# The last feed-forward computes its routed experts only for the chosen pairs, with rows moved by indirect transfers

## The reference, cut to what matters

```
g = x @ sw1.T; u = x @ sw2.T                     # 256 -> 1024 each
shared_out = silu(g) * u @ sw3.T                 # 1024 -> 256
scores = sigmoid(x @ router_w.T)                 # 8 experts
_, top_idx = top_k(scores + expert_bias, 2)
top_scores = scores[top_idx] / (sum + 1e-9)
h12 = einsum('td,ehd->teh', x, w12)              # every expert: 256 -> 128 gate, 128 up
out_e = einsum('teh,edh->ted', silu(h1) * h2, w3)
return shared_out + einsum('ted,te->td', out_e, combine)
```

## Time and profile before

| | us |
|---|---|
| median of 3 runs | 2937.14 (2932.88 to 2939.26) |
| the profiled execution, own time | 2938.26 |
| its span in the trace | 2936.5 |
| gating phase (first work to first work of `l3f`) | 2528.1 to 2565.7 |
| `l3f` | 2565.7 to 2927.5 |
| last transfer and end | 2927.5 to 2936.5 |

### The profile page before, as it was taken

The page is one execution under the profiler, slowest core; times in us unless marked ns, Lnnn a source line. Parts: engine busy times, 40 slices in busy tenths (PEclk is TensorE's granted clock), DMA queues, the critical chain, the costliest instruction groups (busy, mean ns, idle before and its releaser), DMA issues. The chain is left out here.

```text
span 2936.5 us, 38100 instructions
## 1 busy us (share of the span) xinstructions
PE 2489.6 (85%) x11114; PEld 1536.4 (52%) x11141; DVE 1415.7 (48%) x3448; ACT 1055.4 (36%) x3161; POOL 580.9 (20%) x832
## 2 busy tenths in 40 slices
PE   4959999999688688869999999994445888599998
PEld 2437676676455344436666566662223455466665
DVE  4951111111355477746656666666775676511111
ACT  1022222222255255535555555552222555221111
POOL 3712222222132200033333333320000000001100
PEclk8959999999899799989999999997666999699999
DMA  7000000000300000000000000002000000000000
GB/s 275 0 7 6 6 5 5 8 5 3 129 1 0 3 1 0 0 6 1 0 0 0 0 0 0 0 0 102 0 0 3 6 4 4 1 1 0 0 0 29
DMA packets 20484, 44.81 MB, mean 15 GB/s; under 512 B 3520, under 2 KB 16192, under 8 KB 19008
## 3 DMA queue, kind: packets, MB, share of 16 engines
q1 hardware_dynamic: 20416, 43.98, 4.1%
HBM read 41.87 MB, written 2.10 MB: 15 GB/s over the span
## 5 line engine op out<-in xcount | busy, mean ns | idle before, releaser
L808 DVE TENSOR_TENSOR moe_hid<-moe_act_g,moe_pU 128x384 f32<-128x384 f32 x128 | 70.9, 554 | 443.5 <-ACT moe_act_g L780 443.5
L780 ACT ACTIVATE moe_act_g<-moe_pG 128x384 f32<-128x384 f32 x128 | 62.8, 490 | 424.6 <-PE moe_pU L735 424.6
L735 PE MATMUL moe_pG<-big,moe_xT 128*128 128x384 f32 x512 | 187.5, 489 | 4.1 <-POOL moe_xT L702 4.1
L1939 ACT ACTIVATE l2x_prob<-l2x_pS,l2x_nb,l2x_rms_q 128x256 f32<-128x256 f32 x256 | 142.5, 566 | 133.4 <-DVE l2x_nb L2087 133.4
L714 POOL TENSOR_TENSOR moe_hidw<-moe_hid,moe_data_w_all 128x384 f32<-128x384 f32 x128 | 105.7, 826 | 426.8 <-DVE moe_hid L808 420.0
L756 PE MATMUL moe_pO<-big,moe_hT 128*128 128x256 f32 x768 | 186.8, 379 | 0.0
L735 PE MATMUL moe_pU<-big,moe_xT 128*128 128x384 f32 x512 | 186.4, 487 | 0.0
L967 PE MATMUL l2x_pQ<-big,l2x_xT 128*128 128x512 f32 x320 | 155.2, 608 | 13.7 <-POOL l2x_cT L2016 10.9
L756 PEld LDWEIGHTS moe_pO<-big,moe_hT 128*128 128x128 f32 x768 | 136.0, 190 | 13.2
L780 ACT ACTIVATE l3f_act_g<-l3f_pG 128x512 f32<-128x512 f32 x64 | 38.2, 597 | 285.9 <-PE l3f_pU L735 285.9
L2084 DVE TENSOR_REDUCE l2x_negmax<-l2x_pS 128x2 f32<-128x512 f32 x128 | 87.8, 686 | 98.1 <-PE l2x_pS L1828 95.3
(11 more groups left out here) (419 smaller groups left out, 5215.5 us busy)
## 6 DMA issues: line engine op xcount, KB each, us to landing
big<-in_e_gate SPq DMA_DIRECT2D x1, 3072.0 KB, 20.8
big<-in_e_up SPq DMA_DIRECT2D x1, 3072.0 KB, 20.7
big<-in_e_down SPq DMA_DIRECT2D x1, 3072.0 KB, 27.7
moe_lanes<-in_l2f_lanes SPq DMA_DIRECT2D x16, 192.0 KB, 2.8
x_all<-in_x SPq DMA_DIRECT2D x1, 2048.0 KB, 8.3
hyena_aT<-in_ctx SPq DMA_DIRECT2D x4, 512.0 KB, 6.8
hyena_toep_rev<-in_k_rev SPq DMA_DIRECT2D x1, 2048.0 KB, 14.1
big<-in_l_wq SPq DMA_DIRECT2D x1, 2048.0 KB, 7.7
```

Source lines behind the costliest of these rows:

```text
L735: last = pe.matmul(ps[:, 0:chunk], lhsT=xT[p][:, k, :], rhs=w(k, c), start=(k == 0), stop=(k == KC - 1))
L780: act.activation(act_g[c % 2][:], pG[c % 2][:, 0:chunk], ACT.Silu).then_inc(silu_done, 1)
L1939: ins = act.activation(prob[g % 2][:, h, :], pS[j][:, (h % 2) * 2 * P:(h % 2 + 1) * 2 * P], ACT.Exp, scale=rms_q[g][:, h:h + 1], bias=nb[: ...
```

## The change

Phases 1 to 3 become one phase, `phase_l3_ffn`. The shared feed-forward is 64 items of a sequence and a chunk of 256 hidden columns, gate and up side by side in one 512-column product (`f_gu`). Each routed item is a tile of 128 rows that all belong to one expert. There are NT = (4096 + 8 x 127) // 128 = 39 such tiles, whatever the data is. The order of items is fixed: 32 shared items (sequences 0 to 7), 39 routed, 32 shared (sequences 8 to 15). One loop step q of TensorE is: `up(q)`, `turn_routed` of the tile two steps ahead, `turn_hidden(q-1)`, `down(q-2)`; ScalarE and VectorE have matching orders.

Routing runs between the early items: logits at q = 2 to 5, exponential and scores at 6, the two choices at 7 and 8, ranks by matmul at 9 (32 small bf16 matmuls), each row's slot at 10, the owner of each tile at 11, the weights at 12. A DRAM buffer `route_x` of 39 x 128 rows of 1 KB is zeroed. GpSimd then scatters the normalised rows to it by 32 indirect transfers (sequence, choice), 128 rows each. SyncE waits for all 32 and loads the tiles, eight ahead. TensorE reads the tile's owner into a register (`value_load`) and takes the expert's weights at that address. The result goes through `y` to a second buffer, `route_y`. When all 39 tiles are stored, GpSimd gathers two rows per token back by 32 indirect transfers into `yk` (four sequences deep). VectorE's `combine` adds both, weighted; each sequence is then stored by itself. The layer norm keeps all 16 normalised tiles (`XN` = B). Every loop is written out; there is no `Fori` left in this step.

```diff
-def phase_gating3(nc, D, G):
-    NE = 8
-    with Phase(nc, "gate3") as ph:
...
+class NormKept(NormAll):
+    XN = B
...
+    NE, TOPK, CH, NC = 8, 2, 256, 4
+    NT = (B * P * TOPK + NE * (P - 1)) // P
+    EARLY = B // 2
+    FLOOR, XR, YR, GR = -3.0e38, 8, 3, 4
+    items = ([("shared", b, c) for b in range(EARLY) for c in range(NC)] + [("routed", j, 0) for j in range(NT)]
+             + [("shared", b, c) for b in range(EARLY, B) for c in range(NC)])
+    Q, R0 = len(items), EARLY * NC
+    R1 = R0 + NT
+    group = {0: range(4, 8), 1: range(8, 12), 2: range(12, 16)}
+    front = [("x", b) for b in range(4)]
...
+        @block.sync
+        def _(sp):
+            def load(j):
+                sp.dma_start(xg[j % XR][:], dx[j * P:(j + 1) * P, :]).then_inc(xg_in[j % XR], 16)
...
+            sp.dma_start(bias[:], D["L3_expert_bias"].partition_broadcast(P)).then_inc(const_in, 16)
...
+            sp.dma_start(lower[:].bitcast(U16), D["c_lower"]).then_inc(const_in, 16)
+            sp.dma_start(onesb[:].bitcast(U16), D["c_onesb"]).then_inc(const_in, 16)
+            sp.wait_ge(cleared, 1)
+            sp.dma_start(dx.rearrange("(j p) c -> p j c", p=P), zero[:].unsqueeze(1).to_broadcast([P, NT, C])
+                         ).then_inc(zeroed, 16)
+            sp.wait_ge(scattered, 16 * TOPK * B)
+            for j in range(XR):
+                load(j)
+            for j in range(NT):
+                sp.wait_ge(out_read, outs["routed", j] + 1)
+                sp.dma_start(dy[j * P:(j + 1) * P, :], y[j % YR][:]).then_inc(y_out[j % YR], 16)
+                if j + XR < NT:
+                    sp.wait_ge(turned, at["routed", j] + 1)
+                    load(j + XR)
+            for b in range(B):
+                sp.wait_ge(combined, b + 1)
+                sp.dma_start(out[b], G["x_all"][:, b, :]).then_inc(stored, 16)
+            sp.wait_ge(stored, 16 * B)
 
         @block.gpsimd
         def _(pool):
-            front_pool(pool)
-        @block.sync
-        def _(sp):
-            sp.dma_start(bias[:], D["L3_expert_bias"].partition_broadcast(P)).then_inc(const_in, 16)
+            for g in range(B // nm.GROUP):
+                nm.pool(pool, g)
+            pool.wait_ge(zeroed, 16)
+            pool.wait_ge(slotted, 1)
+            for b in range(B):
+                for k in range(TOPK):
+                    pool.indirect_dma_start(dx, bass.IndirectOffsetOnAxis(slot_i[:, k, b:b + 1], 0), nm.xn[b][:],
+                                            None).then_inc(scattered, 16)
+            for r in range(YR):
+                pool.wait_ge(y_out[r], 16 * len(range(r, NT, YR)))
+            for b in range(B):
+                if b >= GR:
+                    pool.wait_ge(combined, b - GR + 1)
+                for k in range(TOPK):
+                    pool.indirect_dma_start(yk[b % GR][:, k, :], None, dy,
+                                            bass.IndirectOffsetOnAxis(slot_i[:, k, b:b + 1], 0)
+                                            ).then_inc(yk_in[b % GR], 16)
         @block.tensor
...
+            def turn_routed(j):
+                bank = place(at["routed", j])
+                pe.wait_ge(xg_in[j % XR], 16 * (j // XR + 1))
+                for k in range(KC):
+                    last = pe.transpose(bank[:, k * P:(k + 1) * P], xg[j % XR][:, k * P:(k + 1) * P], G["ident"][:])
+                last.then_inc(turned, 1)
+            def turn_hidden(q):
+                bank = place(at["hidden", q])
+                _, n = sources(q)
+                pe.wait_ge(hid_done, q + 1)
+                for k in range(n // P):
+                    last = pe.transpose(bank[:, k * P:(k + 1) * P], hid[q % 2][:, k * P:(k + 1) * P], G["ident"][:])
+                last.then_inc(turned, 1)
+            def up(q):
+                kind, i, c = items[q]
+                xT, n = sources(q)
+                if kind == "shared":
+                    cols = slice(2 * CH * c, 2 * CH * (c + 1))
+                    pe.wait_ge(turn_read, at["x", i] + 1)
+                else:
+                    if i == 0:
+                        pe.wait_ge(owners, 1)
+                    expert[i] = pe.value_load(owner_i[0:1, i:i + 1], min_val=0, max_val=NE - 1)
+                    cols = bass.ds(expert[i] * CH + 2 * CH * NC, CH)
+                    pe.wait_ge(turn_read, at["routed", i] + 1)
+                if q >= 3:
+                    pe.wait_ge(hid_done, q - 2)
+                for k in range(KC):
+                    last = pe.matmul(pA[q % 3][:, 0:2 * n], lhsT=xT[k], rhs=W["f_gu"][:, k, cols], start=(k == 0),
+                                     stop=(k == KC - 1))
+                last.then_inc(gu_ps, 1)
+            def down(q):
+                kind, i, c = items[q]
+                o, n = outs[kind, i], sources(q)[1] // P
+                pe.wait_ge(turn_read, at["hidden", q] + 1)
+                if c == 0 and o >= 2:
+                    pe.wait_ge(out_read, o - 1)
+                for k in range(n):
+                    if kind == "shared":
+                        w = W["f_down"][:, c * n + k, :]
+                    else:
+                        w = W["f_down"].rearrange("p k c -> p (k c)")[:, bass.ds(expert[i] * C + C * NC * CH // P, C)]
+                    last = pe.matmul(pO[o % 2][:, 0:C], lhsT=hT[q % 2][:, k, :], rhs=w, start=(c == 0 and k == 0),
+                                     stop=(q == lastq[kind, i] and k == n - 1))
+                last.then_inc(down_done, 1)
...
+            def ranks():
+                n = B * NE
+                pe.wait_ge(const_in, 16 * 6)
+                pe.wait_ge(chosen, 1)
+                pe.matmul(pL[:, n:2 * n], lhsT=lower[:], rhs=selb[:], start=True, stop=True)
+                for d in range(1, B):
+                    pe.matmul(pL[:, n + d * NE:2 * n], lhsT=onesb[:], rhs=selb[:, 0:n - d * NE], start=False, stop=True,
+                              skip_group_check=True)
+                for b in range(B):
+                    last = pe.matmul(pL[:, 2 * n:2 * n + NE], lhsT=onesb[:], rhs=selb[:, b * NE:(b + 1) * NE],
+                                     start=(b == 0), stop=(b == B - 1))
+                last.then_inc(ranked, 1)
...
+            for q in range(Q + 2):
+                if q < Q:
+                    up(q)
+                if R0 <= q + 2 < R1:
+                    turn_routed(q + 2 - R0)
+                if 0 < q <= Q:
+                    turn_hidden(q - 1)
+                for b in group.get(q, ()):
+                    turn_x(b)
+                if q in (2, 3, 4, 5):
+                    for b in range(4 * (q - 2), 4 * (q - 1)):
+                        scores(b)
+                if q == 9:
+                    ranks()
+                if q >= 2:
+                    down(q - 2)
 
         @block.scalar
...
+            def evict_routed(j):
+                t = at["routed", j]
+                act.wait_ge(turned, t + 1)
+                if j >= 2:
+                    act.wait_ge(gu_ps, R0 + j - 1)
+                act.activation(xgT[j % 2][:].rearrange("p k t -> p (k t)"), pT[t % 2][:, 0:C],
+                               ACT.Copy).then_inc(turn_read, 1)
+            def evict_hidden(q):
+                t, n = at["hidden", q], sources(q)[1]
+                act.wait_ge(turned, t + 1)
+                if q >= 2:
+                    act.wait_ge(down_done, q - 1)
+                act.activation(hT[q % 2][:].rearrange("p k t -> p (k t)")[:, 0:n], pT[t % 2][:, 0:n],
+                               ACT.Copy).then_inc(turn_read, 1)
+            def silu(q):
+                _, n = sources(q)
+                act.wait_ge(gu_ps, q + 1)
+                if q >= 2:
+                    act.wait_ge(hid_done, q - 1)
+                act.activation(act_g[q % 2][:, 0:n], pA[q % 3][:, 0:n], ACT.Silu).then_inc(silu_done, 1)
+            for b in range(4):
+                evict_x(b)
+            for q in range(Q + 1):
+                if q < Q:
+                    silu(q)
+                if R0 <= q + 2 < R1:
+                    evict_routed(q + 2 - R0)
+                if q > 0:
...
+                if q == 6:
+                    act.wait_ge(logits, B)
+                    act.activation(score[:].rearrange("p b e -> p (b e)"), pL[:, 0:B * NE], ACT.Exp,
+                                   scale=-1.0).then_inc(exp_done, 1)
...
+            def route_choose(k):
+                counts = count[:].unsqueeze(1).to_broadcast([P, B, NE])
+                ch(dve.tensor_reduce(red[:], pick[:], AX.X, ALU.max))
+                ch(dve.tensor_tensor(coded[:], pick[:], bc(red[:], NE), ALU.is_ge))
+                ch(dve.tensor_tensor(coded[:], coded[:], counts, ALU.mult))
+                ch(dve.tensor_reduce(red[:], coded[:], AX.X, ALU.min))
+                ch(dve.tensor_tensor(per_expert(sel[:, k, :]), counts, bc(red[:], NE), ALU.is_equal))
...
+            def gated(q):
+                _, n = sources(q)
+                dve.wait_ge(silu_done, q + 1)
+                if q >= 2:
```

(50 more changed lines are left out.)

197 lines of the change are left out of this document (143 added, 54 removed).

## The result

The changed kernel takes 2823.28 us (median of 4 runs, 2822.25 to 2831.67), beside 2935.01 us of the kernel before in the same comparison (4 runs, 2930.67 to 2939.26). The ratio is 0.9629, with a 95% interval of 0.9609 to 0.9649: faster, but by 112 us where 205 were forecast, and 23 us above the upper end of the range.

The account below looks back on a forecast made before the run. TensorE's matmuls were taken to bound the kernel. The stage summed as 144 to the tiles' end + 48.3 late items + 4.7 wait + 2 hitches + 4 tail = 203 us for 408.4, giving 2732 us, range 2695 to 2800.

Parts of the forecast that it names:

- one step of the ring: Old feed-forward loop on TensorE: matmuls and transposes of one step, put at 5.60 us, 64 steps 358 us.
- matmuls removed: TensorE's columns in the stage: 358 us of matmuls become 135, at 1.51 us a shared item and 0.98 a routed tile.
- slots: Routing among the early shared items: the rows' slots are ready 42 us after the phase's start.
- pace of the scatter p: GpSimd's time per indirect transfer, taken as 1.3 us, between 0.4 and 2.1.
- standstill in the scatter: Before the first routed tile: TensorE stands 15 us for scattered data, plus 2 us for the fallen clock.
- a tile: Routed items: TensorE needs 0.98 us, with ScalarE and register loading 1.3 us each, 51 us for 39.
- wait of the first combine: Start of the late shared items: VectorE, and TensorE with it, waits 4.7 us for the first gathered sequence.
- The front: From the phase's start to the slots: norms, nine steps, logits, routing operations and ranks, 42 us in sum.
- rival 1: Scatter and gather: indirect transfers go one after another or nearly so, from 1.7 us each; 2778 us at 2.1; chance 0.20.
- rival 4: Scatter and gather: GpSimd makes addresses row by row so slowly the kernel gets slower; 2963 us at 5 us each; chance 0.04.
- rival 2: Scatter: hidden behind the shared items, at most 0.84 us a transfer; 2713 us at 0.43; chance 0.12.
- Rival 3: Routed tiles: the register load stops TensorE in every tile, 2.3 us a tile, 39 us more, 2771 us; chance 0.12.

Follow-up runs that it names:

- e2_pairs: The changed kernel, but GpSimd waits for both landings after every two scatters; 2817.64 us, ratio 0.961.
- e10_half_up_eights: The changed kernel with scatters in groups of eight and one of the two gate-and-up products of each shared item left out; 2768.39 us (one run).
- e6_eights: The changed kernel, but GpSimd waits for all landings after every eight scatters; 2796.21 us (one run), timed again 2805.51 us, ratio 0.9553.
- e3_direct_pool: The changed kernel with its 32 indirect scatters replaced by 32 plain transfers of the same size from GpSimd's queue; 2805.38 us (one run).

## Why the prediction was wrong

**Where it failed: the count of passes in "one step of the ring".** The prediction lists four 512-column matmuls 1.72, transposes 0.44, eight 256-column ones 1.73, "5.60 in all". These add to 3.89; the rest is the second row, `l3f_pU` x4, 1.71. Whoever had added up would have seen that a step has eight records at 512 columns where the code has 2 x 2 products, and eight at 256 where it has four (the description of the ring gives "eight down matmuls", which is the count of records too). The same ratio stands in the logits, four records for a pair of matmuls. The prediction then priced the new items by the code's count and one record's 0.43 and 0.216: 1.51 us for a shared item. Measured are 2.80. For a routed tile it had 0.98, and its price of 1.3 with ScalarE and the register; measured are 1.62.

| term | predicted | measured |
|---|---|---|
| matmuls removed | 358 - 135 = 223 | 358 - (64 x 2.80 + 39 x 1.62 = 242) = 116 |
| slots | 42 | 55.1 |
| pace of the scatter p | 1.3 | 1.27 |
| data in SBUF | 88 | about 100 |
| TensorE wants it | 73 | 107.8 |
| standstill in the scatter | 15 + 2, for data | 25.0, late signals, none for data |
| a tile | 1.3 | 1.62 |
| from the end of the tiles on TensorE to the first gather | 6 | 9 (202.4 to 211.4) |
| wait of the first combine | 4.7 | none; 1.7 of late signals nearby |
| late items | 48.3 | 32 x 2.80 = 89.6 |
| stage | 203 | 300.9 |

The 98 us that the stage is longer than forecast are 64 x 1.29 = 83 for shared items, 39 x 0.32 = 12 for tiles, 8 for the standstill (25 in place of 17), less 3 at the first combine (1.7 in place of 4.7); that is 100, 2 more than the difference, in which roundings and the 2 us forecast for hitches lie. The prediction's form, TensorE's columns plus what stands between, was right. Its first number wasn't, and most others lean on it. A smaller misreading stands ahead of it: of the 40 slices the last five are 9, 9, 9, 9, 8 behind a 5, not eight nines behind a 4; the windows carry the argument without it.

**The front.** 13.1 us late, of which nine steps explain 11.6. VectorE's first product starts at 10.8 us where 9.9 was forecast. The zeroing landed in 16.7 us for 18.5.

**The scatter.** The pace from the row of 1.03 us was right, and rival 1 (landings in turn) and rival 4 are false. But the conclusion turned over, since slower items cover the scatter: rival 2's case (nothing waits for data) came true without its condition, p of 0.84 at most. Where the scatter is slower (e2_pairs) or the cover shorter (e10_half_up_eights), the forecast wait appears, 14.3 and 11.8 us. The Trainium skill (DMA: Bandwidth & Descriptors, section "Anatomy of one DMA — SWDGE (gpsimd) path") names 2.0 us fixed and bytes over 436 GB/s. For 128 KB that gives an estimate of 2.3 us. The landings of this case agree: 2.4 us for a scatter in e6_eights, 2.2 for a plain transfer of GpSimd in e3_direct_pool. The pace doesn't follow, 1.27 us, so the fixed part overlaps between transfers.

**The register.** Rival 3 is false: the tile's 1.62 us are matmuls alone, so `value_load` costs nothing that shows. ScalarE isn't the bound either: it is busy 30.99 of the 67.20 us of the tiles, TensorE 67.20.

**What no step had.** The 25 us of late signals. Neither a row of before nor the prediction has anything of it; they happen to be near the 17 us foreseen in the same place, which hides the miss if one compares sums only.

**What beats both kernels.** The scatter in groups of eight, one wait each: 0.9553 (0.9536 to 0.957) of before against the change's 0.9629 (0.9609 to 0.9649), about 22 us less; groups of four give the same 0.9553. On a chip that shows no late signals there would be little to win by it; no run of the changed kernel is known to be from chip 1, so this isn't shown. What is left of the stage, 271.5 us, is 242 us of matmuls and 29 of front and tail.

## What to carry to other kernels

Before a duration per instruction is taken from a timeline, count the records of one loop step against the products in the code, and add up the step: a sum that doesn't give the distance between steps is a row left out. When work is shortened, price anew what it covered, for a slower or faster step turns the sign of a wait (here the scatter, hidden at 2.80 us a step, bare at 1.94). And an experiment on a step's cost is read at the step, not at the stage's end.

## What the runs showed of the hardware

- One f32 matmul is two records of TensorE and costs twice one record's distance: 0.86 us at 512 columns and granted clock 1.00. Leaving one out makes the step 0.86 us shorter (2.80 to 1.94).
- TensorE's semaphore increments reach ScalarE and VectorE late while GpSimd issues 128-row indirect transfers back to back, from about the ninth on. In the scatter of the changed kernel it is 1.6 us, then 13, then 25, in their order; beside some ten gathers up to 4.6. Increments of ScalarE (0.03 us to VectorE in the same stretch) are not late. It outlasts the transfers: the last landing is seen at 2617.57, the last late signal at 2621.12. It didn't happen in the scatter in groups of 2 and 8, nor with plain transfers at more than twice the pace (0.54 us), on chips that showed it elsewhere in the same execution. The mean DMA share is 0.34 meanwhile, so it isn't simply bandwidth. It isn't always there: on one chip twelve gathers in a row did nothing, and its traces alone hold all landing records of their indirect scatters. Whether 64 rows avoid it, and what the cause is, stays open. All executions of this study were traced, also the timed ones, so whether an execution without a trace has it can't be said; no run separates it.
- An indirect transfer of 128 rows of 1 KB costs GpSimd 1.27 us from one to the next (0.96 busy), of 64 rows 1.21: nearly a fixed price between these two sizes, so the fuller transfer is the cheaper way per row.
- Loading an expert number into a register on TensorE and using it as the weights' address leaves no gap on TensorE at one per 1.62 us.
